# Linear attention between two mixture-of-experts blocks: projections half by half, the tile loop from the second quarter's sums on, squares one step later

## The chip, the cores and the metric

The kernel runs on one core of one Trainium2 chip. The metric is the device time of one execution in microseconds. A core has TensorE (PE, with its weight loads as PEld), VectorE (DVE), ScalarE (ACT), GpSimd (POOL) and SyncE (SP), which work through their own lists of instructions in order and wait for one another by semaphores, and 16 DMA engines. SBUF is the on-chip memory of 128 partitions; PSUM (`ps`) is the memory of eight banks into which TensorE writes.

## The reference, cut to what matters

1024 tokens of width 256, float32 throughout:

```python
x = x + 0.5 * ffn(layernorm(x))       # 16 experts, top 4, width 176; a shared expert, width 704
x = x + attn(layernorm(x))
x = x + 0.5 * ffn(layernorm(x))       # the same weights
# attn: two heads of 128
q = silu(x @ Wq.T);  f = sigmoid(x @ Wk.T);  log_f = log_sigmoid(f);  v = x @ Wv.T
k = 1 - exp(log_f)                    # so k = 1 - sigmoid(f)
S_t = diag(exp(log_f_t)) @ S_{t-1} + outer(k_t, v_t);   o_t = q_t @ S_t
return rmsnorm(o, norm_w) @ Wo.T
```

The recurrence is computed in tiles of 128 tokens: running sums A of log_f, products q·exp(A) and k·exp(-A), a masked 128x128 score matrix, and a state that is carried from tile to tile.

## The kernel before, in words

The program has five stages, one after the other: `ffn(0)`, whose layernorm is `norm(0)`; `norm(1)`, in which `combine` also adds the expert results to X; `attention`; `ffn(1)`, whose layernorm `norm(2)` is woven into the attention's tile loop; and a last `combine`. There is no planner. The order is the order in which each engine's block is written, held together by counting semaphores. An `ffn` first computes router logits, DVE chooses the experts and places (`choose`, `places`), POOL scatters the token rows to slots in HBM by 32 indirect DMAs (`dispatch`, line 710), meanwhile PE, ACT and DVE compute the shared expert in ten "units", and then 47 expert tiles follow.

`norm(c)` takes eight tiles of 128 tokens. DVE (lines 783 to 791) runs `added(t)` (for c = 1 two additions of expert results, lines 917 and 919; in front of tile 4 also the four of line 809), `stats(t)` (lines 775 and 776), and `scale` (line 781), which writes the normalized tile into XR. ACT computes 1/sqrt of the variance for a pair of tiles (`rates`, lines 554 and 556), PE transposes XR (`turned`, line 306) and ACT copies the result into XT (`copied`, line 561). Before the change DVE scales tiles 0 and 1 after the statistics of tile 3, 2 and 3 after those of tile 5, and 4 to 7 at the end. ACT runs the rates of tiles 0 to 3, then copies 0 and 1, the rates of 4 and 5, copies 2 and 3, the rates of 6 and 7, and copies 4 to 7.

In `attention` PE first transposes all eight tiles, then projects keys and then queries (`project`, line 452). One projection is one head and one half of 512 tokens; there are four of keys and four of queries. Then come the values (line 465, 32 pieces), a wait for all four products of the queries, eight bf16 matmuls on a dummy tile (`keep_warm(8, B_KT)`, line 470), and the tile loop. ACT loads the sigmoid table (line 614), runs four sigmoids of the keys (line 620) interleaved with four second sigmoids (line 624), and four of the queries (line 628), then loads the table for logarithm and exponential (line 629). DVE forms K = 1 - E1 (line 940), multiplies the queries (line 944) and the weights (line 946).

The tokens are then treated in quarters of two tiles. ACT takes logarithms (`logs(q)`, line 633); DVE makes running sums and copies the values out of PSUM (`sums(q)`, lines 952 to 964, and `values(q)`, line 968), for all four quarters before its tile loop; ACT takes exponentials (`decays(q)`, lines 639 to 641).

The tile loop, tile t of eight, is spread over the engines. In its iteration i PE runs `turn_k(i)` (476), `kv(i-1)` (491), `scores(i)` (483), `outputs(i-1)` (503, 505), `product(i-2)` (515, 518), and from i = 5 on `turned(2, i-5)` and the logits of `ffn(1)` (312). `product(t)` waits for `added(t-1)`, because both use one PSUM bank (`wait(pe, s_xu, NT + t ...)`). `scores(i)` waits for `masked(i-1)`. DVE runs `masked(i)` (973), `summed(i-1)` (980, 984), `added(i-3)` (990), `stats`, `scale`. `added(t)` waits for `rms(t)` of ACT (664, 666), which waits for `product(t)`. ACT runs `keys` (646), `rates`, `state` (653), `outputs` (660), `copied`, `rms`. POOL runs `grown(i)` (733), `decayed(i)` (738), `squares(i-2)` (743).

## Time and profile before

| what | value |
|---|---|
| median of three runs | 546.1 us (544.96 to 546.13) |
| the profiled execution, its own time | 546.05 us |
| its span, first to last instruction | 544.2 us |
| mean granted TensorE clock, share of full | 0.923 |
| busy share PE, DVE, ACT, POOL | 85%, 44%, 22%, 41% |
| norm(1) and transposes, from 237.2 us to | 254.7 us |
| projections, values, sums, from 254.7 us to | 286 us |
| tile loop and its tail, from 286 us to | 325.4 us |

All times within the execution are counted from the start of the span. The 1.85 us by which the execution's own time is longer than its span lie around it. A shared number such as "PE 85% busy" is a mean over stages that have different limits; the rows below are therefore taken stage by stage.

### The profile page before, as it was taken

The page shows a single profiled execution, that of the slowest core. Times are in us where ns is not written, and L with a number is a line of the kernel's source. Part 1 is how long each engine was busy: PE and PEld are TensorE (multiplying, and loading weights), DVE is VectorE, ACT ScalarE, POOL GpSimd, SP SyncE. Part 2 cuts the span into 40 slices and gives each one's busy share as a digit, 9 for nine tenths or more (in the row PEclk, how much of TensorE's full clock was granted, in tenths as well). Part 3 has the DMA queues.
Part 4 walks back from the last instruction along what each step waited for, and adds up shares of the span by engine and source line. Part 5 has one row for each costly group of instructions (what it writes and reads, how often), then busy time and mean ns, then how long its engine had stood idle before and what let it go on. Part 6 is the DMA issues. An engine that isn't in the chain of part 4 may idle for free.

```text
span 544.2 us, 7022 instructions
## 1 busy us (share of the span) xinstructions
PE 463.1 (85%) x1897; PEld 305.6 (56%) x1898; DVE 239.4 (44%) x708; ACT 122.2 (22%) x352; POOL 225.5 (41%) x188
## 2 busy tenths in 40 slices
PE   6949639899999999955968889990989999999992
PEld 4625315566666666632548874640566666666651
DVE  6551012254444454465394648300234444454436
ACT  3200000122222222123545542100112222222210
POOL 0057720055556555600034302775015666556540
PEclk9979777999999999985988988996799999999996
DMA  8999871178887666550000000323006666666647
GB/s 265 339 396 388 213 273 65 37 163 151 154 156 115 105 103 106 73 153 13 0 1 0 2 2 21 115 107 120 2 21 101 104 118 103 102 104 109 109 52 230
DMA packets 49591, 65.18 MB, mean 120 GB/s; under 512 B 5435, under 2 KB 45243, under 8 KB 48955
## 3 DMA queue, kind: packets, MB, share of 16 engines
q1 hardware_dynamic: 32947, 43.36, 26.2%
q0 software_dynamic: 16608, 21.37, 24.7%
q8 instruction: 18, 0.29, 0.2%
q14 instruction: 18, 0.15, 0.1%
HBM read 30.94 MB, written 33.77 MB: 119 GB/s over the span
## 4 chain that ended last, share of the span: by engine, by line
PE 63%; another core or an unknown queue 9%; DMA 9%; DVE 8%; SPq 5%; issue 5%; ACT 1%; POOL 0%; DVEq 0%; POOLq 0%
PE ps L380 19%; PE ps L398 13%; PE ps L355 6%; PE ps L332 5%; PE ps L387 5%; DMA sums<-ar,idx 4%; PE ps L337 4%; SPq L254 3%; PE ps L366 3%; PE ps L452 3%; DMA WS<-wsh 2%; DMA back<-sums 2%; PE ps L515 2%; DVE X L917 1%
## 5 line engine op out<-in xcount | busy, mean ns | idle before, releaser
L721 POOL DMA_INDIRECT sums<-ar,idx x94 | 145.4, 1547 | 163.8 <-DVE ar L898 109.9
L380 PE MATMUL ps<-W,ar 128*128 x376 | 131.4, 472 | 1.2 <-issue 1.2
L398 PE MATMUL ps<-W,ar 88*128 x376 | 97.0, 380 | 1.4 <-DVE ar L891 1.4
L710 POOL DMA_INDIRECT slots<-XR,pos x64 | 62.8, 982 | 69.5 <-DMA slots<-zeros 30.6
L355 PE MATMUL ps<-WS,ar 128*128 128x256 f32 (+1 forms) x192 | 52.8, 426 | 37.3 <-DVE ar L799 15.3
L885 DVE SCALAR_TENSOR_TENSOR ar<-ps,xs,ar 128x176 f32<-128x176 f32 x94 | 37.7, 401 | 104.2 <-issue 62.5
L380 PEld LDWEIGHTS ps<-W,ar 128*128 128x128 f32 x376 | 63.7, 189 | 25.4 <-issue 1.9
L594 ACT ACTIVATE ar<-ps 128x176 f32<-128x176 f32 x94 | 29.8, 317 | 188.6 <-PE ps L380 186.7
L355 PEld LDWEIGHTS ps<-WS,ar 128*128 128x128 f32 (+1 forms) x192 | 40.1, 213 | 55.0 <-issue 39.0
L398 PEld LDWEIGHTS ps<-W,ar 88*128 88x128 f32 x376 | 64.0, 190 | 7.4 <-issue 1.9
L332 PE MATMUL ps<-XT,WS 128*128 128x512 f32 x96 | 54.1, 692 | 0.0
L898 DVE COPY ar<-ps 128x256 f32<-128x256 f32 x94 | 39.9, 425 | 23.8 <-PE ps L398 19.9
L799 DVE TENSOR_TENSOR ar<-ps,ar 128x512 f32<-128x512 f32 x20 | 13.8, 690 | 82.2 <-remote 31.6
L583 ACT ACTIVATE ar<-ps 128x512 f32<-128x512 f32 (+1 forms) x24 | 14.2, 595 | 148.1 <-PE ps L332 88.6
L387 PE MATMUL ps<-cst,ar 128*88 128x128 f32 x188 | 39.4, 291 | 2.1 <-DVE ar L885 1.7
L366 PEld LDWEIGHTS ps<-cst,xs 128*128 128x128 f32 x188 | 26.3, 141 | 25.1 <-issue 14.0
L337 PE MATMUL ps<-XT,WS 128*128 128x512 f32 x80 | 40.2, 627 | 0.0
L891 DVE COPY ar<-ps 88x256 f32<-88x256 f32 x94 | 38.5, 410 | 1.4 <-PE ps L387 1.0
L589 ACT ACTIVATE ar<-ps 128x256 f32<-128x256 f32 x94 | 36.0, 383 | 10.1 <-PE ps L366 10.0
L366 PE MATMUL ps<-cst,xs 128*128 128x128 f32 x188 | 36.0, 273 | 0.3 <-DMA xs<-slots 0.3
L387 PEld LDWEIGHTS ps<-cst,ar 128*88 128x88 f32 x188 | 15.6, 122 | 27.6 <-DVE ar L885 23.8
L332 PEld LDWEIGHTS ps<-XT,WS 128*128 128x128 f32 x96 | 21.0, 224 | 17.8 <-issue 16.6
(130 smaller groups left out, 383.3 us busy)
## 6 DMA issues: line engine op xcount, KB each, us to landing
xs<-slots SPq DMA_DIRECT2D x94, 138.0 KB
slots<-zeros SPq DMA_DIRECT2D x1, 6486.0 KB, 26.1
W<-w SPq DMA_DIRECT2D x4, 1408.0 KB
back<-sums SPq DMA_DIRECT2D x16, 256.0 KB, 3.0
W<-w SPq DMA_DIRECT2D x1, 2816.0 KB
sums<-zeros SPq DMA_DIRECT2D x2, 1152.0 KB
sums<-zeros SPq DMA_DIRECT2D x18, 128.0 KB
sums<-ar,idx POOLq DMA_INDIRECT x94
```

What stands on the lines that cost most here:

```text
L332: mm = pe.matmul(ps[:, 4 + u % 2, :], WS1[:, k, 2 * j, :], XT[:, k, half(h)], start=k == 0, stop=k == KD - 1)
L337: mm = pe.matmul(ps[:, 6 + u % 2, :], WS1[:, k, 2 * j + 1, :], XT[:, k, half(h)], start=k == 0, stop=k == KD - 1)
L355: mm = pe.matmul(ps[:, 2 * h + i // 2, i % 2 * D:(i % 2 + 1) * D], Hs[u % 2][rows, tok(i)], WS2[rows, j, :], start=first and i % 2 == 0, s ...
L366: mm = pe.transpose(ps[:, i % 2, k * P:(k + 1) * P], xs[i % NX][:, k * P:(k + 1) * P], ident)
L380: mm = pe.matmul(ps[:, 4 + i % 2, 0:2 * FE], xt[i % 2][:, k * P:(k + 1) * P], w, start=k == 0, stop=k == KD - 1)
L387: mm = pe.transpose(ps[0:KE, 6 + i % 2, c * P:(c + 1) * P], hm[i % 2][:, c * KE:(c + 1) * KE], ident)
L398: mm = pe.matmul(ps[:, 2 + i % 2, 0:D], ht[i % 2][:, c * P:(c + 1) * P], w, start=c == 0, stop=c == 1)
L710: pool.indirect_dma_start(out=slots_dram[:, :], out_offset=bass.IndirectOffsetOnAxis(ap=pos[:, t, r:r + 1], axis=0), in_=XR[:, t, :], in_o ...
L721: pool.indirect_dma_start(out=sums_dram[f][a][:, :], out_offset=bass.IndirectOffsetOnAxis(ap=idx[:, i:i + 1], axis=0), in_=ys[i % NY], in_ ...
L885: dve.scalar_tensor_tensor(hm[i % 2], ps[:, 4 + i % 2, FE:2 * FE], row[:, bass.ds(e + R_CF, 1)], sg[i % 2], ALU.mult, ALU.mult).then_inc(s ...
L891: dve.tensor_copy(ht[i % 2], ps[0:KE, 6 + i % 2, 0:D]).then_inc(s_htc, 1)
L898: dve.tensor_copy(ys[i % NY], ps[:, 2 + i % 2, 0:D]).then_inc(s_y, 1)
```

## The change

In words: (a) in `norm`, DVE scales a pair of tiles one tile sooner (0 and 1 after the statistics of tile 2, and so on) and ACT takes the rates of a pair directly behind the copies of the pair before; this holds for `norm(0)` too. (b) PE transposes four tiles, projects the keys of the first half, then transposes the other four in pairs with the first half's two query projections between, and then projects the second half's keys and queries; ACT and DVE follow that order; the sigmoid table is loaded inside `norm(1)`. (c) `keep_warm(8)` goes. (d) DVE enters its tile loop after two quarters' sums and values; the other two quarters come inside iterations 0 and 1. ACT's `decays(3)` follows step 2 and not step 1. (e) In DVE's iteration `added(i-3)` stands ahead of `masked(i)`. (f) POOL squares tile i-3 and not i-2 in iteration i.

```diff
 def attention():                                   # PE
-    for t in range(NT):
-        turned(1, t)
-    for cols, bank, done in ((0, 0, a_kp), (D, 4, a_qp)):
-        for h in range(2):
-            pe.wait_ge(s_xc, NT + (4 * h + 4 if cols == 0 else NT))
-            for e in range(NH):
-                project(h, e, cols, bank, done)
+    def keys_in(h):
+        pe.wait_ge(s_xc, NT + 4 * h + 4)
+        for e in range(NH):
+            project(h, e, 0, 0, a_kp)
+    def query_in(h, e):
+        project(h, e, D, 4, a_qp)
+    for t in range(4):
+        turned(1, t)
+    keys_in(0)
+    for e in range(NH):
+        turned(1, 4 + 2 * e)
+        turned(1, 5 + 2 * e)
+        query_in(0, e)
+    keys_in(1)
+    for e in range(NH):
+        query_in(1, e)
...
     pe.wait_ge(a_q, 4)
-    keep_warm(8, B_KT)
 def norm(c):                                       # ACT
     rates(c, 0, 2)
-    rates(c, 2, 2)
-    for q in range(2, 4):
-        copied(c, 2 * q - 4)
-        copied(c, 2 * q - 3)
+    for q in range(1, 4):
+        copied(c, 2 * q - 2)
+        copied(c, 2 * q - 1)
         rates(c, 2 * q, 2)
-    for t in range(4, NT):
+    if c > 0:
+        act.preload_act_table(ACT.Sigmoid)
+    for t in range(NT - 2, NT):
         copied(c, t)
...                                                # ACT: for each half two sigmoids of the keys,
...                                                # two second sigmoids, two of the queries
     step(1)
+    step(2)
     decays(3)
-    for i in range(2, NT + 5):
+    for i in range(3, NT + 5):
         step(i)
-for i in range(NT + 2):                            # POOL
+for i in range(NT + 3):
     if i < NT:
         grown(i)
         decayed(i)
-    if i >= 2:
-        squares(i - 2)
+    if i >= 3:
+        squares(i - 3)
     stats(c, t)                                    # DVE, norm
-    if t >= 3 and t % 2 == 1:
-        scale(c, t - 3)
+    if t >= 2 and t % 2 == 0:
         scale(c, t - 2)
+        scale(c, t - 1)
...                                                # DVE: the products of the queries half by half
-for q in range(4):                                 # DVE, attention
+for q in range(2):
     sums(q)
     values(q)
 for i in range(NT + 4):
+    if 3 <= i < NT + 3:
+        added(i - 3)
     if i < NT:
         masked(i)
     if 1 <= i < NT:
         summed(i - 1)
+    if i < 2:
+        sums(i + 2)
+        values(i + 2)
     if 3 <= i < NT + 3:
-        added(i - 3)
         stats(2, i - 3)
     if i >= 4:
         scale(2, i - 4)
```

## Rows read from the trace of the kernel before

**Rows 1.** Windows by stage: from:to us, length, then busy us (xinstructions) by engine, clock, DMA.
```profile
236.00:254.70 18.70, 6.34 (x26) 4.41 (x26) 15.25 (x44) 4.91 (x16) 0.00 (x0) 0.65 0.31 98
254.70:286.00 31.30, 25.79 (x84) 14.76 (x83) 17.24 (x37) 16.26 (x30) 4.82 (x6) 0.88 0.00 1
286.00:325.40 39.40, 33.51 (x236) 31.41 (x237) 19.37 (x52) 19.31 (x71) 11.86 (x18) 0.93 0.00 1
```
**Rows 2.** Timeline, DVE in norm(1): start us, us, what [idle before, releaser].
```profile
237.22 0.42 DVE L917 TENSOR_TENSOR X<-X,back 128x256 f32<-128x256 f32 x1 [1.57 <-DMA back<-sums]
...
243.08 0.72 DVE L781 TENSOR_SCALAR XR<-X,mv,rstd 128x256 f32<-128x256 f32 x2
...
251.91 1.42 DVE L781 TENSOR_SCALAR XR<-X,mv,rstd 128x256 f32<-128x256 f32 x4
```
**Rows 3.** Timeline, PE from the first transposes to the values.
```profile
243.58 1.09 PE L306 MATMUL ps<-cst,XR 128*128 128x128 f32 x4 [5.63 <-issue]
...
252.37 2.34 PE L306 MATMUL ps<-cst,XR 128*128 128x128 f32 x8 [2.45 <-DVE XR L781]
254.50 15.89 PE L452 MATMUL ps<-XT,WA 128*128 128x512 f32 x32
...
270.23 7.07 PE L465 MATMUL ps<-WA,XT 128*128 128x256 f32 x32
```
**Rows 4.** Timeline, ACT: the first rates and copies, the two table loads, the first logarithms.
```profile
240.28 0.30 ACT L554 ACTIVATE lnv<-mv,eps_ln 128x2 f32<-128x2 f32 x1 [4.05 <-DVE mv L776]
...
249.52 0.81 ACT L561 ACTIVATE XT<-ps 128x256 f32<-128x256 f32 x2 [0.53 <-PE ps L306]
...
255.15 1.28 ACT L614 ACT_TABLE_LOAD   x1
...
271.04 1.28 ACT L629 ACT_TABLE_LOAD   x1
```
**Rows 5.** Windows of half a microsecond round each change of TensorE's granted clock.
```profile
241.00:241.50 0.50, 0.00 (x0) 0.00 (x0) 0.46 (x2) 0.00 (x0) 0.00 (x0) 0.94 0.75 260
258.50:259.00 0.50, 0.50 (x2) 0.19 (x1) 0.00 (x0) 0.25 (x1) 0.00 (x0) 0.99 0.00 0
282.00:282.50 0.50, 0.00 (x0) 0.00 (x0) 0.50 (x3) 0.09 (x1) 0.02 (x1) 0.90 0.00 0
289.00:289.50 0.50, 0.50 (x5) 0.50 (x5) 0.00 (x0) 0.50 (x3) 0.38 (x1) 0.78 0.00 0
```
**Rows 6.** Timeline, DVE between the projections and the tile loop.
```profile
273.07 1.27 DVE L955 TENSOR_TENSOR_SCAN ar<-steps,ar 128x256 f32<-128x256 f32 x2 [0.80 <-ACT ar L633]
...
274.65 0.42 DVE L961 TENSOR_TENSOR ar<-ar,lf 128x256 f32<-128x256 f32 x1
...
277.58 0.83 DVE L961 TENSOR_TENSOR ar<-ar,lf 128x256 f32<-128x256 f32 x1
...
285.48 0.43 DVE L973 COPY_PREDICATED SM<-cst,ps 128x256 f32<-128x256 int32 x1
```
**Rows 7.** Timeline, PE in the tile loop.
```profile
290.55 1.03 PE L515 MATMUL ps<-WO,OT 128*128 128x256 f32 x4
...
294.60 1.10 PE L515 MATMUL ps<-WO,OT 128*128 128x256 f32 x4 [0.62 <-DVE X L990]
...
311.94 1.10 PE L515 MATMUL ps<-WO,OT 128*128 128x256 f32 x4 [0.62 <-DVE X L990]
...
315.13 1.10 PE L515 MATMUL ps<-WO,OT 128*128 128x256 f32 x4
```
**Rows 8.** Timeline: PE and DVE in ffn(0), POOL in ffn(0), ACT in ffn(1).
```profile
35.13 3.75 PE L355 MATMUL ps<-WS,ar 128*128 128x256 f32 x8 [7.02 <-DMA WS<-wsh]
...
31.79 1.25 POOL L710 DMA_INDIRECT slots<-XR,pos  x1 [30.59 <-DMA slots<-zeros]
...
27.45 0.17 DVE L859 TENSOR_SCALAR pos<-m 128x32 int32<-128x32 f32 x1
...
380.65 0.60 ACT L583 ACTIVATE ar<-ps 128x512 f32<-128x512 f32 x1 [19.76 <-remote]
```

More of the change, by code:

```diff
@@ L613, in attention @@
                 norm(1)
-                act.preload_act_table(ACT.Sigmoid)
-                for i in range(5):
-                    if i < 4:
-                        h, e = i // 2, i % 2
-                        act.wait_ge(a_kp, i + 1)
-                        act.activation(A[:, e, half(h)], ps[:, i, :], ACT.Sigmoid).then_inc(a_sk, 1)
-                    if i > 0:
-                        h, e = (i - 1) // 2, (i - 1) % 2
-                        act.wait_ge(a_sk, i)
+                for h in range(2):
+                    for e in range(NH):
+                        act.wait_ge(a_kp, 2 * h + e + 1)
+                        act.activation(A[:, e, half(h)], ps[:, 2 * h + e, :], ACT.Sigmoid).then_inc(a_sk, 1)
+                    for e in range(NH):
+                        act.wait_ge(a_sk, 2 * h + e + 1)
                         act.activation(E1[:, e, half(h)], A[:, e, half(h)], ACT.Sigmoid).then_inc(a_s2, 1)
-                for i in range(4):
-                    h, e = i // 2, i % 2
-                    act.wait_ge(a_qp, i + 1)
-                    act.activation(Q[:, e, half(h)], ps[:, 4 + i, :], ACT.Sigmoid).then_inc(a_sq, 1)
+                    for e in range(NH):
+                        act.wait_ge(a_qp, 2 * h + e + 1)
+                        act.activation(Q[:, e, half(h)], ps[:, 4 + 2 * h + e, :], ACT.Sigmoid).then_inc(a_sq, 1)
                 act.preload_act_table_set("natural_log_exp_and_others")
@@ L940, in attention @@
                     dve.tensor_scalar(K[:, :, half(h)], E1[:, :, half(h)], -1.0, 1.0, ALU.mult, ALU.add).then_inc(a_K, 1)
-                for i in range(4):
-                    h, e = i // 2, i % 2
-                    dve.wait_ge(a_sq, i + 1)
-                    dve.tensor_tensor(Q[:, e, half(h)], ps[:, 4 + i, :], Q[:, e, half(h)], ALU.mult).then_inc(a_q, 1)
+                    for e in range(NH):
+                        dve.wait_ge(a_sq, 2 * h + e + 1)
+                        dve.tensor_tensor(Q[:, e, half(h)], ps[:, 4 + 2 * h + e, :], Q[:, e, half(h)], ALU.mult).then_inc(a_q, 1)
                 for k in range(NH):
```

## The prediction

> **What bounds the kernel now.** I read the slices of the page first, then the windows by stage, then the chain of waits, and last the timeline of each engine where the chain turned. The change touches three stages in a row and nothing after them but by shifting it.
>
> The windows [rows 1] show three limits. From 236 to 254.7 us DVE is busy 15.25 of 18.7 us and PE 6.34: the stage is DVE's. From 254.7 to 286 us PE is busy 25.8 of 31.3 us, but that is a mean over two halves: the projections run without a gap from 254.50 to 270.4 us and the values from 270.23 on [rows 3], and from 273.07 to 285.48 us it is DVE's sums and values for which the first mask waits [rows 6]. From 286 to 325.4 us PE has 33.5 of 39.4 us of work, and the reader should see that the rest is not spread evenly: product(1) starts with 0.62 us of idle time behind line 990 and product(5) too [rows 7]; products 2, 3 and 4 between them have the same row, five in all. The clock is not full: it falls at 241.5 us, 3.5 us after PE's last matmul of the first block, rises at 258.5, 4 us after the dense projections began, falls again about 282.4 and rises at 289.2 [rows 5]. The two low stretches answer to the two stretches in which PE waits for DVE.
>
> **The change part by part.** The profiled execution took 546.05 us, the median of the three runs (546.1) to 0.05, so differences from its rows apply to the median directly. It is 1.85 us longer than its span; that part stays.
>
> *The norm's order and the projections.* DVE's additions and statistics take 1.46 us a tile from 237.22 us (two tiles of two additions, statistics and aggregate, repeated eight times; three are done at 241.62). The rates of tiles 0 and 1 start at 240.28 and take 0.53 [rows 4], so they are ready, and the first two scales stand at 241.62 in place of 243.08 [rows 2], 1.46 sooner. Tile 3 and the four additions of line 809 follow; the second pair of scales moves from 248.34 to 246.88, again 1.46 sooner. From a pair's scale to the end of its copies into XT the second pair took 2.0 us (to 250.33 [rows 4]), so XT's first half is complete at 248.9 and keys_in(0) can start at 249.0; before, the first projection came at 254.7 behind all eight transposes [rows 3]. That is 5.7 us sooner. But the clock is low there. At low clock a projection took 3.43 us (254.7 to 258.1, which ACT's first sigmoid of the keys saw at 258.16), at full clock 1.72 (the last seven from about 258.5 to 270.4). The clock rose 4 us after dense work began [rows 5]; I put it at 253 us. Then the first two projections end at 254.2: one at 3.43, the second about 1.8. Transposes 4 and 5 add 0.55 us; their XR exists from 251.1. The query projection (0,0) runs to 256.5.
>
> Here stands a new wait. ACT takes the rates of tiles 6 and 7 behind the copies of 4 and 5, and these wait for PE, which transposes 4 and 5 only behind keys_in(0). So these rates end at 255.8, DVE's last two scales at 256.5, where before they were done at 253.3 [rows 2]. Queued behind them on DVE is nothing until K, on ACT the table load (1.28 us, as at 255.15 [rows 4]) and copies 6 and 7, which end at 257.7. PE is covered by query (0,0) until 256.5, transposes 6 and 7 to 257.05, query (0,1) to 258.8; copy 7 is there 1 us before the second half's keys need it. Four more projections of 1.72 end at 265.7. Before, they ended at 270.4. PE therefore gives 4.7 us. ACT follows: the first half's six sigmoids (0.52 to 0.62 each) run from 257.7 to 261, the second half's last waits for PE at 265.7 and the table load stands at 266.35 against 271.04 [rows 4]: 4.7 again. DVE's first sum moves from 273.07 to 268.4. The values end at 272.7. I take 4.7; with the clock rising 1.5 us sooner or later than put it is 5.5 to 4; with the whole first half at low clock (two more projections at 3.43 and not 1.72) it would be 2.5.
>
> *The entry of the loop.* All from here is on the new time. Sums and values of two quarters took 6.5 us of the 12.4 between 273.07 and 285.48 [rows 6], so masked(0) stands at 274.85; scores(0) is ready at 274.0. Then sums(2) and values(2): unhindered a quarter is 2.0 + 0.6 us, beside POOL's products it was 3.3 + 0.6 (the subtraction of line 961 takes 0.42 alone and 0.83 while POOL multiplies [rows 6]). POOL is then at grown and decayed of tiles 1 to 3, so I take 3.3: masked(1) at 279.05, summed(0) to 279.75. ACT's decays(2) ends at 279.65 and keys(1), queued behind it, at 279.95: PE's turn_k(2) cannot start before 280.05. sums(3) and values(3) cost 3.1: masked(2) at 282.85, summed(1) to 283.8, state(2) to 284.5.
>
> The keep_warm matmuls go: before, 8 of them stood between the values and turn_k(0) (1.5 us) and DVE was later than both, so by themselves they cost nothing and give nothing. PE's work is now thin from 274 to 280 us (1.6 us in 6) and the clock will be low at 280, as it was at 282.4 after a thinner stretch of 2 us [rows 5]. PE from 280.05: turn_k(2), kv(1), scores(2), outputs(1) at half clock, 4.1 us, to 284.15; product(0) to 285.3, with the clock rising within it. turn_k(3), kv(2), scores(3), outputs(2) at full clock 2.05: product(1) starts at 287.35. Its other conditions are met: rms(0) ends at 285.8, and added(0), first now in DVE's iteration 3, at 286.25. decays(3), behind rms(0) on ACT, delays keys(3) to 287.3, and turn_k(4) needs that at 288.65 only. Before, product(1) started at 294.60 [rows 7]. So 7.25 us by there, 2.55 of them from the entry. If the clock stays up at 280 the entry gives about 4; if it rises 2 us later or sums(3) too are slowed to the full 3.9, about 1.
>
> *added ahead of masked.* Before, PE waited in every iteration: masked, summed, added one after another on DVE, then product. Between product(0), that did not wait (290.55, 0.22 after the matmul before it), and product(1), that did, the difference is the idle 0.62 plus the tail of the pipeline, 0.78 us by the weight loads. Now added(i-3) needs only rms(i-3), which ends 0.65 us after product(i-3), or 1.25 where a copy of `copied` stands before it on ACT; PE has turn_k, kv, scores and outputs to do first (2.05 us, and 0.6 of transpose and logits in the later ones), so the wait is gone and what is late next is PE itself: 4.12 us an iteration becomes 3.34. masked(i) behind added(i-3) is at worst 0.3 us later and is needed 2 us later. Products 2 to 5 each save 0.78: 3.1. Product(6) saves nothing: it started 3.19 after product(5) [rows 7] by the round of rms, added and product, and that round is the same. The tail to the last logits is the same round twice more. Bounds: 0 (if each iteration has another wait of that size) to 3.1.
>
> *squares a step later, decays(3) a step later.* POOL has 2.0 us of work in an iteration of 3.34. squares(t) now stands behind grown(t+3) and decayed(t+3), that is 1.4 us later than possible, and is needed over 3 us later. Zero; if that cover failed, 0.6 us an iteration.
>
> *norm(0).* The same order costs there, since PE is quick: turned(2), (4), (6) now wait for a copy, two rates and a scale. The round from turned(3) to turned(4) is 2.1 us and was 1.17. Summed from the first rows it makes the logits 2.1 us later. The places (27.45 us) would be there at 29.6; POOL's dispatch waits for the fill of the slots until 31.79 and PE for weights until 35.13 [rows 8]. Hidden by both; were they not, +2.1.
>
> Sum: 4.7 + 2.55 + 3.1 = 10.35. 546.05 - 10.3 = 535.7 us.
>
> In ffn(1) all shifts together, also ACT's wait of 19.8 us [rows 8], whose releaser the profile does not know; it ends 4 us after the last dispatch, in ffn(0) 5 after. ACT's list has the same number of instructions ahead of it as before.
>
> The Trainium skill ("GPSIMD Engine Reference", Specifications) says GpSimd shares VectorE's SBUF interfaces, and that DVE instructions with two SBUF inputs contend. That speaks against moving sums beside POOL's products, and line 961's doubling agrees. With unslowed sums the entry would give 1.3 us more.
>
> **The rivals.** *The front gives half*: low clock through the whole first half or the new wait for rates of 6 and 7 reaching PE. It speaks for it that PE is nearly idle up to 249. 4.7 becomes 2.5: 538. *The clock does not fall at the entry*: against it, 282.4. 534. *The loop has a next wait*, ACT's chain state, outputs, copied, rms, keys of which 2.5 us fill 3.34: the 3.1 go, 538.8. *The change does not do what it says*: masked(1) behind sums(2) and keys(1) behind decays(2) make the loop start no sooner than before relative to the sums, and the loop has its next wait: only 4.7 is left, 541.4. *Slower*: the low clock stays. Without keep_warm and with thin work from 274 us, PE enters the loop at half clock; if the small matmuls with gaps do not lift it, an iteration costs 3.34 more; from the fourth iteration at low clock on (3 x 3.34 is about the 10.3) it is slower than before, and all eight give +16, 562 us. Against: before, the same matmuls lifted it after 3.2 us (286.06 to 289.2 [rows 5]), and my iterations have no gap. The Trainium skill ("TensorE: Matmul & The Clock Gate", HAM oscillation) warns of just this, a kernel cold anew at each round because PE waits in each; the loop before waited in each and stayed at full clock.
>
> **How the numbers follow.** Forecast 0.60; front half 0.13; clock up at the entry 0.10; loop's next wait 0.08; no more than the front 0.04; slower 0.05. The likeliest's own range is 533.5 to 538. The first four give 532.5 to 540, which leaves out about 0.1 above and little below. About 0.2% is what a measurement of this kernel can tell from no change. The slower case also holds 0.01 that ends within 0.2%: faster 0.95, same 0.01, slower 0.04.
>
> **What would show it.** Right: the first projection at 249 us, the second sigmoid table load near 266.3, masked(0) near 275, product(1) near 287.4 at 3.34 us from product(2), product(5) near 301.6, ffn(1) units from 315.1, the dispatch of ffn(0) still at 31.8. Wrong: a new idle group before lines 452 or 476 of more than 1 us, product still idle behind `added`, a low clock past 290 us.

## The result and the profile after

| | before | changed |
|---|---|---|
| median | 546.07 us (544.96 to 546.13, 4 runs) | 534.25 us (528.23 to 539.32, 4 runs) |
| profiled execution, its span | 546.05, 544.2 us | 531.96, 530.1 us |
| mean granted clock | 0.923 | 0.935 |
| PE, DVE, ACT, POOL busy | 85, 44, 22, 41% | 86, 45, 23, 43% |

The ratio is 0.9712, with a 95% interval of 0.965 to 0.9774. Runs more than 1.5% above the fastest of a kernel are left out of every ratio here, which favours a kernel whose runs scatter, so that this one leaves out 536.55 and 539.32 us and stands for about 530.3 us. By the ratio the kernel became faster by 15.7 us, between the profiled executions by 14.1, by the medians of four by 11.8; a further six runs of the changed kernel (first experiment) say 15.0. The forecast was 10.35.

The windows by stage, changed kernel (columns as in [rows 1]):
```profile
234.00:246.50 12.50, 3.83 (x16) 2.47 (x15) 11.06 (x32) 2.53 (x8) 0.00 (x0) 0.72 0.46 134
246.50:277.00 30.50, 27.42 (x92) 16.90 (x93) 19.91 (x46) 17.64 (x38) 6.38 (x8) 0.89 0.00 0
277.00:311.20 34.20, 30.67 (x228) 29.23 (x229) 20.19 (x57) 18.86 (x71) 10.75 (x16) 0.95 0.01 2
```
The stage that is DVE's alone has shrunk from 18.7 us [rows 1] to 12.5, since the projections no longer wait for its end. In the loop PE is busy 30.67 of 34.2 us, before 33.51 of 39.4: what went is 2.4 us of idle time and 2.8 us of busy time at the entry, where matmuls ran at half clock or now stand ahead of the window.

The timeline of PE, changed kernel; these answer to [rows 3]:
```profile
246.50 5.25 PE L450 MATMUL ps<-XT,WA 128*128 128x512 f32 x8 [0.47 <-ACT XT L572]
251.59 0.60 PE L306 MATMUL ps<-cst,XR 128*128 128x128 f32 x4
252.02 1.88 PE L450 MATMUL ps<-XT,WA 128*128 128x512 f32 x4
...
262.77 7.07 PE L476 MATMUL ps<-WA,XT 128*128 128x256 f32 x32
```
The first row is the first half's two key projections: they start 11.71 us after the first addition of norm(1) and take 5.25 us. From there to the end of the values no row of PE shows a wait.

DVE and ACT in the same stretch, changed kernel ([rows 2], [rows 4] and the first of [rows 6]):
```profile
234.79 0.42 DVE L926 TENSOR_TENSOR X<-X,back 128x256 f32<-128x256 f32 x1 [1.46 <-DMA back<-sums]
...
253.12 0.73 DVE L790 TENSOR_SCALAR XR<-X,mv,rstd 128x256 f32<-128x256 f32 x2 [2.90 <-ACT rstd L567]
...
265.61 1.27 DVE L963 TENSOR_TENSOR_SCAN ar<-steps,ar 128x256 f32<-128x256 f32 x2 [0.80 <-ACT ar L641]
```
```profile
253.10 1.28 ACT L581 ACT_TABLE_LOAD   x1
...
263.58 1.28 ACT L637 ACT_TABLE_LOAD   x1
```
The 2.90 us in front of 253.12 are the new wait that was foreseen: DVE's last scales wait for rates behind copies behind transposes behind projections. No row of PE or ACT shows a wait for it in turn. The first sum stands 7.46 us sooner than at 273.07 [rows 6]. Of these, 2.43 are there already at the first addition (234.79 against 237.22 [rows 2]), that is, before anything in norm(1) has run.

The clock round its changes, half-microsecond windows of the changed kernel ([rows 5]):
```profile
249.50:250.00 0.50, 0.50 (x2) 0.19 (x2) 0.47 (x2) 0.00 (x0) 0.00 (x0) 0.84 0.00 0
273.50:274.00 0.50, 0.50 (x5) 0.50 (x4) 0.50 (x1) 0.00 (x0) 0.50 (x2) 0.55 0.00 0
276.50:277.00 0.50, 0.00 (x0) 0.00 (x1) 0.50 (x2) 0.50 (x3) 0.45 (x1) 0.54 0.00 0
277.00:277.50 0.50, 0.47 (x4) 0.50 (x5) 0.50 (x2) 0.50 (x3) 0.00 (x0) 1.00 0.00 0
308.00:308.50 0.50, 0.50 (x3) 0.50 (x4) 0.29 (x1) 0.18 (x1) 0.00 (x0) 0.50 0.00 0
```
At the entry of the loop the clock is at its lower level (1.2 GHz) from 273.5 to 277.0 us only; before, it was so from 282.4 to 289.2. In the tail it falls at 307.7 (the window from 307.5 to 308.0 shows 0.68), 10.1 us after product(5); before, at 323.4, 11.4 us after it. Both times it stays down for 6.8 us.

DVE at the entry and PE in the loop, changed kernel ([rows 6], [rows 7]):
```profile
272.08 0.42 DVE L981 COPY_PREDICATED SM<-cst,ps 128x256 f32<-128x256 int32 x1
272.41 1.78 DVE L963 TENSOR_TENSOR_SCAN ar<-steps,ar 128x256 f32<-128x256 f32 x2
...
275.86 0.44 DVE L981 COPY_PREDICATED SM<-cst,ps 128x256 f32<-128x256 int32 x1
...
280.64 0.42 DVE L981 COPY_PREDICATED SM<-cst,ps 128x256 f32<-128x256 int32 x1
```
```profile
281.71 0.68 PE L502 MATMUL ps<-back,Kt 128*128 128x128 f32 x4 [1.00 <-DVE xs L992]
...
283.61 1.10 PE L526 MATMUL ps<-WO,OT 128*128 128x256 f32 x4
...
286.95 1.03 PE L526 MATMUL ps<-WO,OT 128*128 128x256 f32 x4
...
297.60 1.03 PE L526 MATMUL ps<-WO,OT 128*128 128x256 f32 x4
...
300.71 1.10 PE L526 MATMUL ps<-WO,OT 128*128 128x256 f32 x4
...
303.90 1.10 PE L526 MATMUL ps<-WO,OT 128*128 128x256 f32 x4 [1.12 <-DVE X L998]
```
Products 1 to 5 carry no idle time any more. Products 1 and 2 stand 3.34 us apart, where they stood 4.13 with 0.62 of idle time; from product(1) to product(5) it is 13.99 us, before 17.34. The row at 281.71 is a wait that the forecast did not have: PE stands 1.00 us for `summed(1)`, since DVE's mask in front of it came late (280.64). Product(7) waits 1.12 us for `added`: the round of the tail, as before.

ScalarE in the units of the shared expert, changed kernel: three of ffn(0) and one of ffn(1) ([rows 8]):
```profile
45.42 0.60 ACT L595 ACTIVATE ar<-ps 128x512 f32<-128x512 f32 x1 [4.56 <-issue]
50.95 0.60 ACT L595 ACTIVATE ar<-ps 128x512 f32<-128x512 f32 x1 [4.93 <-PE ps L332]
75.57 0.59 ACT L595 ACTIVATE ar<-ps 64x512 f32<-64x512 f32 x1 [24.03 <-remote]
...
367.24 1.08 ACT L595 ACTIVATE ar<-ps 128x512 f32<-128x512 f32 x2 [19.06 <-remote]
```
The kernel before has in ffn(0), in the places of the second and third of these rows:
```profile
56.35 0.60 ACT L583 ACTIVATE ar<-ps 128x512 f32<-128x512 f32 x1 [9.31 <-remote]
77.44 1.07 ACT L583 ACTIVATE ar<-ps 64x512 f32<-64x512 f32 x2 [20.50 <-remote]
```
"Remote" means that the profile knows no releaser. Before, ScalarE was held twice, from 47 and from 57 us on; in this execution of the changed kernel once for long, from 51.5 us on. The first expert tile starts at 100.51 us, not 102.46.

The marks used from here on are the first addition of norm(1), DVE's first sum, product(1), product(5), and the places of ffn(1), DVE's last step before the dispatch; "the tail" is the stretch from product(5) to the places. From mark to mark the 14.1 us of the profiled pair divide so: ffn(0) and its combine 2.43, front 5.03, entry to product(1) 3.53, products 1 to 5 3.35, the rest until the places of ffn(1) -0.15, all behind them -0.1.

### The profile page after: what moved, and what is told of

The parts are those of the page before. It is cut to its first block, busy times and chain, and to the rows that moved or that the text cites. A ratio compares the mean times of both kernels' runs of the same rounds, so it can differ in the third digit from the quotient of the medians.

```text
span 530.1 us, 7008 instructions
## 1 busy us (share of the span) xinstructions
PE 457.2 (86%) x1890; PEld 302.8 (57%) x1890; DVE 239.2 (45%) x708; ACT 120.7 (23%) x352; POOL 226.6 (43%) x188
## 4 chain that ended last, share of the span: by engine, by line
PE 69%; DVE 7%; another core or an unknown queue 6%; DMA 5%; issue 5%; SPq 5%; ACT 1%; POOL 0%; DVEq 0%; POOLq 0%
PE ps L380 22%; PE ps L398 15%; PE ps L355 7%; PE ps L387 5%; PE ps L332 5%; PE ps L337 4%; PE ps L366 4%; SPq L254 4%; PE ps L450 3%; DMA WS<-wsh 2%; DMA back<-sums 2%; DMA sums<-ar,idx 1%; PE ps L526 1%; DVE ar L963 1%
## 5 line engine op out<-in xcount | busy, mean ns | idle before, releaser
L606 ACT ACTIVATE ar<-ps 128x176 f32<-128x176 f32 x94 | 29.8, 317 | 189.0 <-PE ps L380 186.6
L332 PE MATMUL ps<-XT,WS 128*128 128x512 f32 x96 | 52.4, 673 | 0.0
L907 DVE COPY ar<-ps 128x256 f32<-128x256 f32 x94 | 39.9, 425 | 23.3 <-PE ps L398 20.4
L387 PE MATMUL ps<-cst,ar 128*88 128x128 f32 x188 | 39.4, 291 | 2.1 <-DVE ar L894 1.9
L366 PEld LDWEIGHTS ps<-cst,xs 128*128 128x128 f32 x188 | 26.4, 141 | 24.4 <-issue 14.0
L337 PE MATMUL ps<-XT,WS 128*128 128x512 f32 x80 | 38.8, 608 | 0.0
```

Source lines behind the costliest of these rows:

```text
L332: mm = pe.matmul(ps[:, 4 + u % 2, :], WS1[:, k, 2 * j, :], XT[:, k, half(h)], start=k == 0, stop=k == KD - 1)
L337: mm = pe.matmul(ps[:, 6 + u % 2, :], WS1[:, k, 2 * j + 1, :], XT[:, k, half(h)], start=k == 0, stop=k == KD - 1)
L366: mm = pe.transpose(ps[:, i % 2, k * P:(k + 1) * P], xs[i % NX][:, k * P:(k + 1) * P], ident)
L387: mm = pe.transpose(ps[0:KE, 6 + i % 2, c * P:(c + 1) * P], hm[i % 2][:, c * KE:(c + 1) * KE], ident)
L907: dve.tensor_copy(ys[i % NY], ps[:, 2 + i % 2, 0:D]).then_inc(s_y, 1)
```

## The experiments

Theory A: the gain of norm(1) and the loop is the forecast's, about 10 us, and what is above it comes from the order in norm(0) by way of ScalarE's wait. Rival B: the norm(0) order is nothing, and what is above it is the clock's or the entry's. Each set of runs was made on one chip, with the kernel before beside it. Two kinds of chip turned up: on some ScalarE is held in the units (before: 544 to 546 us), on others never (before: 514 us).

**Chip with the wait: the order in norm(0) and the front alone.** The changed kernel again, no edit:

> The changed kernel once more, to see a second trace and more times. The first trace is 14.1 us shorter than the one of before, and 2.4 us of that are gained before the first addition of norm(1) (234.79 us against 237.22), where I had priced the change at nothing. Theory A, the gain of ffn(0) belongs to the changed program: it stands again at 234.8 us within 0.5, and the time is 532 within 1. Theory B, the length of ScalarE's unexplained wait during the dispatch differs from execution to execution in this program: the first addition stands somewhere between 232 and 242 us, the times again spread over some 10 us, and the attention between first addition and last logits stays at 75.9 us (310.6 less 234.8) within 2.

Measured: 530.91 us (6 runs), ratio 0.9723 (0.9679 to 0.9767); before beside it 545.87. The first addition of norm(1) stands at 230.29 us, outside what either theory allowed, and ScalarE is held twice, not once:
```profile
62.63 0.59 ACT L595 ACTIVATE ar<-ps 64x512 f32<-64x512 f32 x1 [9.73 <-remote]
78.07 1.08 ACT L595 ACTIVATE ar<-ps 128x512 f32<-128x512 f32 x2 [14.85 <-remote]
```
So the length of ffn(0) varies between executions of the changed kernel, and the 2.43 us of the pair on record are one draw. Norm(0) put back in the changed kernel:
```diff
 def norm(c):                      # ACT, and DVE alike
+    # for c == 0: rates of 0 to 3, copies 0 and 1, rates of 4 and 5, ...
```


> The changed kernel with the old order of scales and rates in norm(0) alone. In the changed kernel the logits of ffn(0) are 2.3 us later than before, the dispatch starts at 32.3 us, where before it started at 31.8, and ScalarE's long wait ends at 75.6 and not 77.4. Theory A (the later logits of norm(0) move the shared units against the dispatch, and this is where the 2.4 us come from): logits end near 17.4 us again, the first addition of norm(1) stands at 237.2, the times spread by 1 to 2 us as before the change, and the median is near 534.3 (546.1 less the 11.8 us gained from there on). Theory B (nothing of norm(0) matters, the wait is a property of each execution): the same scatter as the changed kernel, 528 to 539.

Measured: 534.56 us, 0.9792 (0.9745 to 0.9839), first addition at 236.83 us, as theory A of this run had it. And the new order in norm(0) alone, in the kernel before:
```diff
 def norm(c):                      # ACT, and DVE alike
+    # for c == 0: copies 2q-2 and 2q-1, then the rates of 2q, ...
```


> The kernel before with the new order in norm(0) alone. Theory A: the first addition of norm(1) at 234.8 us, a time near 543.7 and a spread that the kernel before did not have. My prediction on record: no difference, 546.1 within 0.5, because the dispatch waits for the fill of the slots until 31.8 us anyway. Theory B: no systematic shift, but any program can scatter; a spread of 10 us here would belong to this order.

Measured: 543.84 us (12 runs, 535.78 to 546.93), 0.9892 (0.9846 to 0.9938), first addition at 234.62 us, again as theory A had it. By the medians the order is worth 3.7 us in the changed kernel and 2.0 in the one before; the ratio of the last stands for 5.9. The intervals of the first two overlap, so the size is loose; the sign is the same in both kernels. ScalarE with the old order in norm(0), in the otherwise changed kernel:
```profile
46.67 0.60 ACT L605 ACTIVATE ar<-ps 128x512 f32<-128x512 f32 x1 [4.56 <-issue]
56.29 0.60 ACT L605 ACTIVATE ar<-ps 128x512 f32<-128x512 f32 x1 [9.03 <-remote]
77.38 1.07 ACT L605 ACTIVATE ar<-ps 64x512 f32<-64x512 f32 x2 [20.49 <-remote]
```
and with the new order in the kernel that is otherwise the one before:
```profile
46.36 0.60 ACT L594 ACTIVATE ar<-ps 128x512 f32<-128x512 f32 x1 [4.56 <-PE ps L332]
52.07 0.60 ACT L594 ACTIVATE ar<-ps 128x512 f32<-128x512 f32 x1 [5.11 <-PE ps L332]
76.00 0.59 ACT L594 ACTIVATE ar<-ps 64x512 f32<-64x512 f32 x1 [23.33 <-issue]
```
The hold from 47 us on goes with the order and with nothing else of the change: one more activation passes before ScalarE is held. All traces of such chips bear it out. With the old order (two traces) the first hold begins at 47.0 and 47.3 us, ScalarE is held 29.8 and 29.5 us in all, and the first addition stands at 237.22 and 236.83. With the new one (seven traces, either kernel) it begins at 51.3 to 53.1 us, comes once or twice, lasts 19.1 to 26.4 us in all, and the first addition stands at 230.2 to 234.8 (mean 232.4). The start of the dispatch does not decide it: 32.29 us in the changed kernel, 32.23 in the same with the old order. B's first half falls on this chip.

The front with norm(0)'s new order, but loop, decays, squares and `keep_warm` as before:
```diff
-for q in range(2):
+for q in range(4):
     sums(q)
     values(q)
...
-    if 3 <= i < NT + 3:
-        added(i - 3)
...
+keep_warm(8, B_KT)
```


> The changed kernel with the tile loop as before (all four quarters' sums ahead of it, added behind summed, decays(3) after step 1, squares of i-2, keep_warm): only the order of norm and of the projections is new. By my terms the front gives 4.7 us: the first sum of VectorE 35.85 - 4.7 = 31.1 us behind the first addition of norm(1) (before 273.07 - 237.22 = 35.85), product(5) 74.72 - 4.7 = 70.0 us behind it (before 311.94 - 237.22). The trace of the changed kernel says 30.8 for the first sum, so 5.0 for the front. Rival: part of what I count to the front is given back at the loop's entry, because the clock or ScalarE's order decides there: product(5) at more than 71 us. Time: 546.1 - 5.0 = 541.1 and whatever ffn(0) does (538.7 if its 2.4 us come along).

Measured: 540.79 us (12 runs, 532.42 to 543.36), 0.9839 (0.9786 to 0.9891). First sum 30.36 us after the first addition, product(5) 69.98 (expected 70.0), with the old 0.62 of idle time in front of products 1 to 5. By the trace the front is there without the loop's part; the times are too scattered to divide the rest.

**Chip without the wait: the parts of entry and loop.** All four sums first (`decays(3)` behind step 1 again with them):
```diff
-for q in range(2):
+for q in range(4):
     sums(q)
     values(q)
...
-    if i < 2:
-        sums(i + 2)
-        values(i + 2)
```


> The changed kernel with all four quarters' sums and values ahead of the tile loop again (and decays(3) after step 1). Counted from the first addition of norm(1), the changed kernel has product(1) at 48.8 (first trace) or 49.4 us (second), product(5) at 62.8 or 63.3. My theory (the entry is worth about 2.5 to 3.5 us, the rest of the gain is the front's 5 and 0.78 for each of four products): product(1) about 52 us, product(5) about 66, the time 3 us over the changed kernel's. Rival (the early loop entry gives nothing, because PE and ScalarE wait for decays(2) and keys(1) just the same): product(5) at 63 to 64 us.

Measured: 506.81 us, 0.9858 (0.9832 to 0.9884). Its DVE timeline has
```profile
254.88 1.27 DVE L962 TENSOR_TENSOR_SCAN ar<-steps,ar 128x256 f32<-128x256 f32 x2 [0.80 <-ACT ar L641]
...
267.28 0.43 DVE L980 COPY_PREDICATED SM<-cst,ps 128x256 f32<-128x256 int32 x1
```
12.4 us from the first sum to the first mask, where the changed kernel has 6.47, and product(5) 67.48 us after the first addition, where it has 64.12 to 64.72 on such chips. `added` behind `masked` and `summed`:
```diff
-    if 3 <= i < NT + 3:
-        added(i - 3)
     if i < NT:
         masked(i)
...
     if 3 <= i < NT + 3:
+        added(i - 3)
         stats(2, i - 3)
```


> The changed kernel with added(i-3) back behind summed(i-1). My theory: every iteration from the third on waits again, the distance from product(1) to product(5) is 17.3 us as before the change (4.05 + 4.13 + 4.12 + 4.35 + 4.74 less the first one), where the changed kernel has 13.9 or 14.0; the time is 3.1 to 3.9 us over the changed kernel's. Rival (the wait moves to the next thing anyway, the loop is bound by a round over ScalarE): less than 1 us.

Measured: 507.09 us, 0.9883 (0.9849 to 0.9917). Its PE timeline:
```profile
271.74 1.10 PE L526 MATMUL ps<-WO,OT 128*128 128x256 f32 x4 [0.62 <-DVE X L998]
275.87 1.10 PE L526 MATMUL ps<-WO,OT 128*128 128x256 f32 x4 [0.62 <-DVE X L998]
280.00 1.10 PE L526 MATMUL ps<-WO,OT 128*128 128x256 f32 x4 [0.62 <-DVE X L998]
```
The idle 0.62 and the 4.13 us an iteration are back by that one line of order; product(1) to product(5) takes 17.35 us (expected 17.3), while the tail is 22.86 us and not 24.9, so that less of it is seen in the time than the 3.1 to 3.9 us expected. `keep_warm(8, B_KT)` back:
```diff
 pe.wait_ge(a_q, 4)
+keep_warm(8, B_KT)
```


> The changed kernel with the eight dummy matmuls back behind the values. My theory: nothing, within 0.5 us: they run while PE would wait for POOL's first Kg and the mask is VectorE's; the clock falls afterwards all the same, because the thin stretch comes after them. Rival: they keep the clock up through scores(1) to outputs(0), which ran at half clock in the first trace (273.5 to 277.0) and also in the second (269.4 to 276.3), and product(1) comes 0.5 to 2 us sooner. Second rival: they delay turn_k(0) and with it the first mask by up to 1 us.

Measured: 504.86 us, 0.9824 (0.9798 to 0.985). In its trace product(1) stands 20.66 us after the first sum, where the seven traces of the changed loop without the dummies have 18.0 to 19.2, and the tail is 1.4 us shorter (23.51, against 24.9 in the other traces of the changed loop on such chips): the dummies do cost at the entry there, and the tail hides it. POOL's squares a step early, as before:
```diff
-    if i >= 3:
-        squares(i - 3)
+    if i >= 2:
+        squares(i - 2)
```


> The changed kernel with POOL's squares one iteration earlier, as before the change. My term: 0 within 0.3 us for the whole loop. Rival: grown and decayed of tile i+1 wait behind squares(i-2), which in the faster loop waits for ScalarE's copy of the outputs, and PE waits for Kg: 0.3 to 0.6 us an iteration, 2 to 4 us in all.

Measured: 504.15 us, 0.9817 (0.9789 to 0.9845). The changed kernel itself was not run on this chip; it took 505.1 us on two other chips of the kind (below). By that, and against 504.15, the late sums give 1.7 to 2.7 us, `added` 2.0 to 2.9, and `keep_warm` and the squares nothing that can be told from the times. The comparison with 504.15 is the surer, being from one chip.

**Another chip without the wait: does norm(0) give anything there?** The kernel before, the changed one, and both with the other order in norm(0):

> The kernel before once more, for a trace from the chip that also runs the next three. The eight runs so far came from two chips: on the first, ScalarE stood once or twice for 10 to 24 us in each dispatch (the trace names no releaser) and the kernel before took 546; on the second there was no such wait, the units of the shared expert followed each other at 5.16 us, and it took 514. Theory (the wait belongs to the chip, and my forecast of norm(0) holds where it is absent): on a chip without the wait the first slot turn of ffn(0) waits for the dispatch and the loads behind it, near 85 us, in this kernel and in all with the new norm(0) order alike, within 1 us.

> The changed kernel on the same chip. If the chip has no such wait of ScalarE: by my terms (4.7 front, 2.55 entry, 3.1 loop, 0 elsewhere) 10.3 us less than the kernel before beside it, the variants of the last call suggest 9.4 to 9.7 (504.2 with the squares moved back, against 513.8). Rival: a further 2 us from norm(0) as on the first chip, 12 in all. If the chip has the wait: 14 to 15 less, as before.

> The kernel before with the new order in norm(0) alone, on the same chip as the kernel before. Without ScalarE's wait: same within 0.5 us (my forecast of the term), or up to 0.5 us slower by the later dispatch (32.3 to 32.7 against 31.8 us in the first chip's traces). With the wait: 2 to 4 us faster, the unit in which the wait begins is one later.

> The changed kernel with the old order in norm(0). Without ScalarE's wait: the changed kernel's time within 0.5 us. With it: 2 to 4 us slower than the changed kernel.

Measured, before beside them 514.2: 513.82 (0.9988), 505.06 (0.9818, 0.9782 to 0.9854), 514.04 (0.9988, 0.997 to 1.0005) and 504.15 us (0.9807). Where ScalarE is not held, the order of norm(0) is worth nothing that can be told in either kernel (0.2 and 0.9 us, both against the new order), and the change gives 9.1 us.

**Does the held ScalarE hang on the dispatch?** On a chip with the wait, dispatch(0) was kept back until the shared expert was done:
```diff
 pool.wait_ge(s_pos, f + 1)
+if f == 0:
+    pool.wait_ge(s_uh, FRONT)
```


> The changed kernel with the dispatch of ffn(0) held back until the ten units of the shared expert are multiplied, to see what ScalarE's wait hangs on. If the chip is one that has the wait, and the wait belongs to the dispatch (it began 14 to 25 us after the dispatch's start and ended 1 to 5 us after its last issue in all traces of that chip, in both ffn): the units of ffn(0) follow each other at 5.16 us without a gap and are done near 78 us, while in ffn(1), where nothing was changed, the wait is there. If the wait belongs to the unit or to the time: it is there in ffn(0) too. The time itself is about 40 us longer, because the dispatch of 41 us no longer lies beside the units. On a chip without the wait the run says nothing on it.

Measured: 560.09 us (2 runs), 1.0344. POOL and ACT in ffn(0):
```profile
78.91 1.15 POOL L721 DMA_INDIRECT slots<-XR,pos  x1 [77.71 <-DVE ar L810]
```
```profile
51.09 0.60 ACT L595 ACTIVATE ar<-ps 128x512 f32<-128x512 f32 x1 [4.56 <-PE ps L332]
56.25 0.59 ACT L595 ACTIVATE ar<-ps 64x512 f32<-64x512 f32 x1 [4.56 <-PE ps L332]
...
388.18 0.60 ACT L595 ACTIVATE ar<-ps 128x512 f32<-128x512 f32 x1 [17.64 <-remote]
```
No unit of ffn(0) is held any more, while in ffn(1) of the same execution, where the dispatch runs beside the units as ever, ScalarE is held for 17.64 us. So the wait in the units needs the dispatch beside them. Its releaser is still not known. (The time was expected 40 us longer; it is 29 to 30.)

**Clock.** bf16 matmuls on the dummy tile where PE idles, first in norm(1) only, then also at the entry and in the tail:
```diff
+keep_warm(16, 0)
 for t in range(4):
     turned(1, t)
+    if t == 1:
+        keep_warm(18, 0)
```


> The changed kernel with dummy bf16 matmuls in PE's two empty stretches of norm(1): 16 ahead of the first transpose (3.4 us into a gap of 4.1) and 18 between the second and the third (3.8 us into a gap of 4.1). It prices the low clock under keys_in(0), which I had bounded and not known: the two projections took 5.25 us in every trace and would take 3.43 at full clock. Theory: the first sum of VectorE moves from 31.1 us (mean of nine traces, counted from the first addition of norm(1)) to 29.3, the time falls by 1.8 us. Rival: the rates of tiles 6 and 7, which stand on ScalarE behind copies 4 and 5, or VectorE's own statistics of tile 7 (done at 15.3 us) set the second half's start, and less than 1 us is gained; or the dummies themselves come in the way of a transpose, then it is 0 or slower.

Measured: 530.13 us, 0.9751 (0.9655 to 0.9848); before beside it 544.23 (536.62 to 548.07). The first sum stands 28.90 us after the first addition, 2.2 us sooner than the mean of the changed kernel's traces (31.15). The second:
```diff
     scores(i)
+    if i == 0: keep_warm(7, B_Y)
     outputs(i - 1)
+    if i == 1: keep_warm(3, B_Y)
...
+    if 8 <= i < NT + 4: keep_warm(4, B_KT)
```


> The same with dummy matmuls also in the loop's entry (7 behind scores(0), 3 behind outputs(0)) and in its tail (4 in each of iterations 8 to 11). In the eight kernels with the new loop the distance from product(7) to the places of ffn(1) is 17.0 to 18.6 us and was 16.1 to 16.8 before the change, the longer the sooner the clock falls in the tail. Theory (the clock took back what my sum had over): product(1) at 48 or sooner less the front's 1.8, the tail at 16.5, in all 3 to 5 us less than the changed kernel. Rival (in the tail VectorE and ScalarE set the pace, the clock is only coincident): no more than e13 gives.

Measured: 525.7 us, 0.9691 (0.9604 to 0.9778). The front with the old loop once more on that chip:

> The changed kernel with the tile loop as before, once more, beside the others of this call. My front term is 4.7 us; nine traces against four give 4.1 for VectorE's first sum. On a chip where ScalarE does not stand during the dispatch: 4 to 5 us less than the kernel before. On a chip where it does, the same and 2 to 3 us from norm(0)'s order.

Measured: 534.16 us, 0.9828 (0.972 to 0.9936), which is 10 us below the kernel before; its trace has the first sum at 31.61 us and product(5) at 71.84, 1.9 us later than the trace above and beyond the 71 us that the rival there had named, so one trace prices a part of the front to about 1 or 2 us only. The spread is too wide there to part 2 us, so the fillers and the changed kernel ran once more on a chip without the wait:

> The changed kernel with fillers for TensorE ahead of the first transposes of norm(1), behind the second of them, behind scores(0) and outputs(0), and in the last four iterations of the loop. Theory (each stretch of low clock ahead of product(5) and in the tail costs what its busy time adds): first sum 28.9 after the first addition against 31.1, product(5) 62.2 against 63.5, places of ffn(1) 85.2 against 88.1, so about 3 us less than the changed kernel beside it, 0.6% of the time. Rival (the fillers give nothing behind the loop, since the router's last steps are DVE's and POOL's): within 1 us of the changed kernel.

> The changed kernel as it is, on the chip of the run with the fillers. Both theories: about 0.982 of the time before where ScalarE does not wait for ten and more us within ffn(0), about 0.972 where it does; it is there to be compared with the fillers on one chip.

Measured, before beside them 514.17: 502.91 us (0.9786, 0.9761 to 0.9811) with fillers, 505.1 us (0.9808, 0.9774 to 0.9843) without. Windows of the changed kernel there (norm(1), loop, behind it):
```profile
224.00:235.80 11.80, 2.43 (x10) 1.38 (x8) 11.05 (x32) 2.54 (x8) 0.00 (x0) 0.60 0.36 116
...
263.90:300.40 36.50, 32.92 (x223) 31.23 (x222) 22.36 (x65) 20.17 (x73) 12.78 (x19) 0.83 0.00 1
300.40:313.00 12.60, 12.60 (x37) 7.60 (x36) 7.79 (x42) 3.62 (x7) 0.00 (x0) 0.69 0.00 1
```
and with fillers:
```profile
223.40:234.70 11.30, 9.05 (x43) 4.01 (x42) 10.68 (x31) 2.41 (x8) 0.00 (x0) 1.00 0.37 117
...
263.00:297.50 34.50, 31.43 (x238) 28.23 (x238) 21.86 (x61) 20.22 (x74) 10.72 (x16) 1.00 0.01 1
297.50:309.00 11.50, 9.20 (x31) 4.55 (x30) 8.44 (x45) 3.23 (x6) 0.00 (x0) 1.00 0.00 0
```
With fillers the clock is full in all three stretches. First sum 28.91 us after the first addition (31.36 without), product(5) 61.89 (64.12), places 84.86 (89.03). This is the fastest version found: 2.2 us in the medians and 3.2 in the spans, with intervals that overlap.

## Why the prediction was right or wrong

The direction and the mechanism in norm(1) and the loop were right. The size was not: 14 to 16 us instead of 10.35, with a range that ended at 532.5 where the comparison stands for 530.3. The table has its steps, counted from the first addition of norm(1), which takes out what happened earlier. The last column is from the means of four traces with the front and loop of before and seven with those of the change:

| step | forecast | profiled pair | means of the traces |
|---|---|---|---|
| first projection | 11.78 us | 11.71 | 11.70 to 11.72 |
| first two projections | 5.2 us | 5.25 | 4.8 to 6.0 |
| front, by the first sum | 4.7 | 5.03 | 4.1 (means 35.25, 31.15) |
| entry, first sum to product(1) | 2.55 | 3.53 | 3.9 (22.47, 18.54) |
| products 1 to 5 | 3.1 | 3.35 | 3.4 |
| product(5) to places of ffn(1) | 0 | -0.15 | -1.7 (22.74, 24.46) |
| all before norm(1) | 0 | 2.43 | 4.6 with the wait, none without |

*The front* is right within 0.6 us. The new wait of DVE came as put, and the clock rose 3.2 us after the projections began, put at 4. The rival of half a front falls: it needed four projections at half clock.

*The entry* was under-sized by 1 to 1.4 us, inside its bounds of 1 to 4. The forecast had the masks 6.45, 10.65 and 14.45 us after the first sum; they came at 6.47, 10.25 and 15.03. Two terms were off, in opposite directions. The clock was put as low until 285, that is 16.6 us after the first sum, and rose 11.4 after it, so that product(0) came 2.3 us sooner than put. And `sums(3)` with its values was put at 3.1 us and took 4.1, beside POOL's products (276.52 to 280.64); this made the third mask late, and PE's 1.00 us at 281.71 with it. The rival that the clock does not fall is wrong as well, it fell at 273.5.

*`added` ahead of `masked`* is right: idle time gone, 3.34 us an iteration, and the one-line reversal brings back 0.62 and 4.13. The rival of a next wait falls. *Squares, `keep_warm`*: nothing in the times, as put; but that the dummies cost nothing held only for the kernel before, where DVE was later, and with the new entry product(1) came 1.5 to 2.7 us later with them. `decays(3)` was moved only together with the sums, so no run prices it.

The Trainium skill ("GPSIMD Engine Reference", Specifications) was cited for GpSimd's interfaces, shared with VectorE. This trace agrees: a pair of scans takes 1.27 us while POOL is idle, and 1.78 at 272.41 and 1.56 at 276.52, beside POOL's products. That the interfaces are the reason no run isolates.

*The tail* was put at zero. On a chip without the wait, product(5) to places is 22.74 us before and 24.91 changed: the clock falls 6.3 us after product(5) (at 293.2 us), against 12.5 before (309.1), and the last logits and first units run at half of it. With fillers the stretch is 22.97. So 2 of the 11.4 us won by product(5) were given back there, and likewise in the first experiment, on a chip with the wait (24.91). In the pair on record they were not (23.35). Among the eight traces with the new loop and no dummies the fall comes 6.3 to 6.5 us after product(5) in six, with 24.9 us to the places, and 10.1 in two, with 23.3, while product(7) follows product(5) by 6.3 us in all. Why the clock falls sooner in some is not shown.

*"Slower, the low clock stays"* fell: PE entered the loop at half clock and the clock rose at 277.0 under the small matmuls, as it had done at 289.2 [rows 5]. The Trainium skill ("TensorE: Matmul & The Clock Gate", HAM oscillation) warns of matmuls between DMA waits that run at a low clock again and again; the loop does not show it, with its waits of 0.62 us (before) or without.

**The step that failed** is norm(0): "Hidden by both". By what it considered, it is true: the logits do come later (places 29.69 us, not 27.45), dispatch starts at 32.29 (31.79), and on a chip where ScalarE is not held the order gives nothing either way. But ScalarE's wait in the units was taken as a constant, one that "shifts" since its list has the same number of instructions ahead of it. That holds in ffn(1), where places to end took 208.8 to 209.8 us in the nine traces of both kernels and their variants on such chips in which both dispatches run beside the units. In ffn(0) it is no constant. How many activations pass before one is caught depends on what ran in norm(0), and here one more passed. That made ffn(0) shorter by 2.0 to 7.0 us in the traces (4.6 in the mean), and the time shorter by 2.0 and 3.7 us by the medians of the two reversals. A wait without known releaser that stands on the path must have a term with both signs in the sum, and a width in the range; with plus or minus one unit (5.16 us) the range would have held the result.

How sum and result meet: without the wait the means give 4.1 + 3.9 + 3.4 - 1.7 = 9.7, measured 9.1, forecast 10.35. The two traces from one such chip give less at the front (3.0 + 3.4 + 3.5 - 2.2 = 7.7 by the places), lose 0.2 ahead of norm(1) and have 1.1 more behind the places, 8.6 in all, so the parts are good to about 1 us. That the forecast lies near 9.1 is in part luck: an entry and a loop larger than put, and a tail given back. With the wait 4.6 more from ffn(0) make 14.3, measured 15.0 and 15.7. In the profiled pair 14.1 - 10.35 = 3.75 us stand over the forecast: 2.43 of ffn(0) and its combine, and 1.56 by which front, entry and loop were larger than put, less 0.25 in what follows.

Left open: what releases ScalarE, why only some chips hold it, and why the norm(0) order lets one more activation pass. Also how much of the remaining 0.7 to 1.4 us above this sum is scatter: before spreads over 8 us on such chips (541.27 to 549.09 in 23 runs).

## What to carry to other kernels

Where a consumer waits once in every iteration for one engine's list, moving that engine's one releasing instruction to the front is worth the idle time plus the tail of the pipeline (0.62 + 0.16 us), and can be costed from one pair of rows. Splitting a projection by halves so that it starts under the norm pays even at half clock. But count each change from the nearest mark ahead of it, on more than one chip: a gain of 2.4 us stood before the first changed instruction of the stage for which it was meant.

## What the runs showed of the hardware that was not expected

- The kernel before took 544 to 546 us in three sets of runs and 514 us in three others (546.07, 545.87, 544.23; 513.82, 514.2, 514.17). What differs in the traces is ScalarE, held for 7 to 24 us at a time in each of the two shared experts, always beside the 32 indirect DMAs of the dispatch; not held without them (51.09 and 56.25 above). Of the 32.5 us between the spans of the kernel before on the two kinds (544.2 and 511.7), 15.3 lie ahead of norm(1) and 16.6 behind the places of ffn(1). The last release comes between 0.3 us before the start of the last of them and 5.6 after it.
- The eight matmuls of the first half's key projections took 4.8 to 6.0 us where the clock rose within them, and 3.70 with the clock held full by fillers.
- What a stretch of full clock gives can be lost again later: on one chip the changed kernel had 13.6 us at half clock behind product(6) (293.2 to 306.8), the one before 3.4 (309.1 to 312.5). In the pair on record both had 6.8.
